# Second expert phase of a two-layer mixture-of-experts kernel: blocks of 288 rows in split F32R, with casting DMAs for the high weight halves

## What is computed

```python
x = x + L0_ffn(L0_cond(x, ...))     # attention with 16 heads, then 16 experts of capacity 128
x = x + L1_ffn(L1_cond(x, ...))     # gated experts over all rows, then the phase of this change

def L1_ffn(x, w_router, w1, b1, w2, b2):        # 8 experts, 256 -> 1024 -> 256, top 2
    probs = softmax(xf @ w_router)
    topk_w, topk_idx = top_k(probs, 2)
    weights = sum(topk_w[..., None] * one_hot(topk_idx, 8), axis=1)
    h = gelu(einsum('te,ieh->tih', xf, w1) + b1)          # tanh form
    out = einsum('tih,ihe->tie', h, w2) + b2
    return sum(out * weights[..., None], axis=1)
```

## Time and profile before

| | us |
|---|---|
| three runs | 954.21, 956.26, 960.77 (median 956.26) |
| the profiled execution, its span from the first to the last instruction | 958.2 |
| PE busy with matmuls | 751.5 (78%) |
| DVE busy | 373.4 (39%) |
| ACT busy | 272.7 (28%) |
| POOL busy | 269.9 (28%) |
| second expert phase, first block's matmul to the last result | 671.58 to 939.07 |

### The profile page before, as it was taken

How to read it: one execution, slowest core, us unless ns; L and a number is a source line. 1 busy time by engine, 2 the same in 40 slices (tenths; PEclk the granted TensorE clock), 3 DMA queues, 4 the chain that set the end, 5 groups by cost and what they waited for, 6 DMA issues and landing times. The chain is left out here.

```text
span 958.2 us, 15240 instructions
## 1 busy us (share of the span) xinstructions
PE 751.5 (78%) x4300; PEld 660.9 (69%) x4301; DVE 373.4 (39%) x1016; ACT 272.7 (28%) x743; POOL 269.9 (28%) x533
## 2 busy tenths in 40 slices
PE   1458777620589999368999999954999999999991
PEld 1357666620479889336888888824999999999991
DVE  3353534458511111196666666646111111111110
ACT  1213414410023233141112111110444544454441
POOL 1122021100034545240001001005444554455442
PEclk9675665555679999787999999987899999999996
DMA  8362191030049996369010010020142454222223
GB/s 257 72 149 44 31 325 49 0 104 7 0 120 318 294 322 169 86 223 324 17 33 16 16 33 17 0 88 6 29 118 50 112 126 123 36 33 38 38 33 104
DMA packets 76904, 94.89 MB, mean 99 GB/s; under 512 B 7856, under 2 KB 68272, under 8 KB 76592
## 3 DMA queue, kind: packets, MB, share of 16 engines
q1 hardware_dynamic: 64000, 77.67, 26.1%
q0 software_dynamic: 10240, 14.32, 8.7%
q10 hardware_dynamic: 2640, 2.62, 0.9%
HBM read 78.39 MB, written 18.10 MB: 101 GB/s over the span
## 5 line engine op out<-in xcount | busy, mean ns | idle before, releaser
L1039 PEld LDWEIGHTS npH<-nXT,w_sb 128*128 128x128 f32 x1152 | 136.4, 195 | 3.2 <-DVE nXT L1070 1.1
L1039 PE MATMUL npH<-nXT,w_sb 128*128 128x128 f32 x1152 | 136.9, 278 | 0.7 <-DVE nXT L1070 0.7
L1047 PE MATMUL npY<-w_sb,nhT 128*128 128x256 f32 x576 | 133.6, 385 | 0.0
L1058 ACT ACT_TABLE_LOAD x40 | 51.3, 1283 | 256.6 <-PE npH L1039 175.6
L1047 PEld LDWEIGHTS npY<-w_sb,nhT 128*128 128x128 f32 x576 | 106.5, 190 | 15.8
L102 POOL TENSOR_TENSOR held<-ones 128x1 f32<-128x1 f32 x212 | 46.0, 217 | 156.2 <-DVE nyg L1087 66.4
L1336 PE MATMUL low_banks<-dw,hid 128*128 128x256 f32 x320 | 77.5, 386 | 4.6 <-DVE hid L1371 4.6
L1058 ACT ACTIVATE nhT<-npH,c_sb 128x128 f32<-128x128 f32 x288 | 78.2, 383 | 0.4
L1310 PE MATMUL f_pt<-xparts,gparts 128*128 128x512 f32 x240 | 72.0, 436 | 2.8 <-ACT uparts L1343 2.8
L1336 PEld LDWEIGHTS low_banks<-dw,hid 128*128 128x128 f32 x320 | 61.5, 193 | 15.5 <-DVE hid L1371 5.4
L1386 DVE SCALAR_TENSOR_TENSOR xc<-low_banks,W,xc 128x256 f32<-128x256 f32 x160 | 66.1, 475 | 2.3 <-PE low_banks L1336 2.3
(11 more groups left out here) (323 smaller groups left out, 965.4 us busy)
## 6 DMA issues: line engine op xcount, KB each, us to landing
w_sb<-in_w SPq DMA_DIRECT2D x32, 1024.0 KB, 8.1
w_sb<-in_v SPq DMA_DIRECT2D x16, 1024.0 KB, 9.8
bias_sb<-in_bias SPq DMA_DIRECT2D x4, 1024.0 KB, 13.3
acc<-zrow SPq DMA_DIRECT2D x1, 2056.0 KB, 17.0
sums<-acc SPq DMA_DIRECT2D x4, 514.0 KB, 5.4
x_sb<-in_x SPq DMA_DIRECT2D x1, 2048.0 KB, 10.1
table<-row ACTq DMA_DIRECT2D x1, 2048.0 KB, 15.5
b_sb<-in_b SPq DMA_DIRECT2D x1, 2048.0 KB, 8.6
```

Source lines behind the costliest of these rows:

```text
L1039: ins = pe.matmul(pH[:, c // 4, (c % 4) * P:(c % 4 + 1) * P], w1_sb[:, u, k, c * P:(c + 1) * P], XT[:, k], start=(k == 0), stop=(k == KD - 1))
L1047: ins = pe.matmul(pY[:, 0:D], hT[:, c], w2_sb[:, u, c], start=(c == 0), stop=(c == FC - 1))
L1058: act.activation(hT[:, c], pH[:, c // 4, (c % 4) * P:(c % 4 + 1) * P], act_fn, bias=b1t[:, ds(e, 1), c]).then_inc(gelu_done, 1)
```

## The change

The second expert phase gets a body of its own in place of expert_phase. The tiles of the dense stage are freed before it.

- Blocks are of WIDE = 288 rows, gathered as NSUB = 3 parts of SUB = 96. The three routing tables have 96 lanes and 75 columns; block numbers come from rounding in f32 instead of integer shifts. In routing, the gate product moves from POOL to ACT, and `ends` goes.
- The transposed form is kept: the weights are stationary in both layers, 288 rows are the moving columns. Each product is three F32R matmuls (low x high, high x low, high x high), in the second layer with w2l, w2h, hh and hl into pY. POOL's scatter(j) waits for yg_ready and issues three DMAs, gather three; gated(j) on DVE waits for y_turned and signals yg_ready. The result is yT (256 wide as 2 x 128 partitions, 288 columns), gets its bias on ACT (Identity), is turned back on PE (turn_back) in the middle of the next block's first layer, and is gated on DVE (gated).
- The hidden tile is split on DVE into hh and hl, two chunks at a time; the gathered columns into xh (ACT) and xl (DVE).
- The weights get four new tiles, w1h, w1l, w2h, w2l, each with two halves for the experts e and e + 1. The high halves of expert 0 are made by ACT (keep_high). Those of experts 1 to 7 are read from HBM a second time by DMAs on POOL's queue that cast f32 to F32R (cast_high). The low halves are made by DVE (low_first, low_second) from the f32 weights in the ring and the high halves. SP reloads a ring slot once the low halves of its expert are made.

```diff
+        def cast_high(pool, e):
+            pool.dma_start(w1h[:, e % 2], v1[e].rearrange("(k p) f -> p k f", p=P)).then_inc(w_cast, 16)
+            pool.dma_start(w2h[:, e % 2], v2[e].rearrange("(c p) d -> p c d", p=P)).then_inc(w_cast, 16)
+        def high_is_there(eng, e):
+            if e:
+                eng.wait_ge(w_cast, 32 * e)
+                eng.wait_ge(w_in[e % RING], 32 * (W_ROUND + 1 + e // RING))
+            else:
+                eng.wait_ge(w_hi, 2)
+        def low_first(dve, e):
+            high_is_there(dve, e)
+            dve.tensor_tensor(w1l[:, e % 2].rearrange("p k f -> p (k f)"), w1_sb[:, e % RING].rearrange("p k f -> p (k f)"),
+                              w1h[:, e % 2].rearrange("p k f -> p (k f)"), ALU.subtract).then_inc(w_lo, 1)
...
+            def per_block(eng, name, body, begin=None):
+                for e in range(E1):
+                    if begin:
+                        begin(eng.snap(reg), e)
+                    n = eng.value_load(nblk[0:1, e:e + 1], min_val=0, max_val=WBLK)
+                    with eng.If(n > 0):
+                        with eng.Fori(0, n):
+                            body(eng.snap(reg), e)
+                            eng.reg_add(reg, reg, 1)
...
+                def _(sp):
+                    sp.sem_inc(gelu_done, FC)
+                    for s in (fc2_done, y_biased):
+                        sp.sem_inc(s, 1)
+                    for e in range(E1 - RING):
+                        sp.wait_ge(w_lo, 2 * e + 2)
+                        load_expert(sp, v1, v2, e + RING, e)
...
+                def _(pool):
+                    gather(0)
+                    cast_high(pool, 1)
+                    pool.dma_start(held[:, 1:2], ones[:, 0:1]).then_inc(scattered, 16)
+                    pool.wait_ge(scattered, 16)
+                    pool.wait_ge(turned, 1)
+                    pool.wait_ge(gathered, 16 * NSUB)
+                    gather(1)
+                    def body(j, e):
+                        scatter(j)
+                        pool.wait_ge(turned, j + 2)
+                        pool.wait_ge(gathered, j * (16 * NSUB) + 32 * NSUB)
+                        held_here(pool, 1)
+                        gather(j + 2)
+                    def begin(j, e):
+                        if 1 <= e and e + 1 < E1:
+                            pool.wait_ge(fc2_done, j + 1)
+                            pool.tensor_tensor(marks[:, e:e + 1], ones[:, 0:1], ones[:, 0:1], ALU.mult)
+                            cast_high(pool, e + 1)
...
+                def _(pe):
+                    def begin(j, e):
+                        pe.wait_ge(w_lo, 2 * e + 2)
+                    def body(j, e):
+                        u = e % 2
+                        pe.wait_ge(x_ready, j + 1)
+                        for c in range(FC):
+                            if c == FC // 2:
+                                turn_back(j)
+                            pe.wait_ge(gelu_done, j * FC + c + 5)
+                            for k in range(KD):
+                                at = slice(c * P, (c + 1) * P)
+                                pe.matmul(pH[:, c % 4, 0:WIDE], w1l[:, u, k, at], xh[:, k], start=(k == 0), stop=False)
+                                pe.matmul(pH[:, c % 4, 0:WIDE], w1h[:, u, k, at], xl[:, k], start=False, stop=False)
+                                ins = pe.matmul(pH[:, c % 4, 0:WIDE], w1h[:, u, k, at], xh[:, k], start=False, stop=(k == KD - 1))
+                            ins.then_inc(fc1_done, 1)
+                        pe.wait_ge(yg_ready, j + 1)
+                        turn(j + 1)
+                        for c in range(FC):
+                            if c % 2 == 0:
+                                pe.wait_ge(h_ready, j * (FC // 2) + c // 2 + 1)
...
+                        ins.then_inc(fc2_done, 1)
...
+                def _(act):
+                    def body(j, e):
+                        for c in range(FC):
+                            act.wait_ge(fc1_done, j * FC + c + 1)
+                            act.activation(h[:, c], pH[:, c % 4, 0:WIDE], ACT.Gelu_apprx_tanh,
+                                           bias=c1_sb[:, e, c:c + 1]).then_inc(gelu_done, 1)
+                        columns(j + 1)
+                        act.wait_ge(fc2_done, j + 2)
+                        act.activation(yT[:, 0], pY[:, 0, 0:WIDE], ACT.Identity, bias=c2_sb[:, e, 0:1])
+                        act.activation(yT[:, 1], pY[:, 1, 0:WIDE], ACT.Identity, bias=c2_sb[:, e, 1:2]).then_inc(y_biased, 1)
...
+                def _(dve):
+                    dve.memset(yT[:], 0.0).then_inc(y_zero, 1)
+                    low_first(dve, 0)
+                    columns(0)
+                    low_second(dve, 0)
+                    def begin(j, e):
+                        if e + 1 < E1:
+                            low_first(dve, e + 1)
+                            low_second(dve, e + 1)
+                    def body(j, e):
+                        for p in range(FC // 2):
+                            if p == FC // 4:
+                                gated(j) 
+                            two = slice(2 * p, 2 * p + 2)
+                            dve.wait_ge(gelu_done, j * FC + 2 * p + 2 + FC)
+                            dve.tensor_copy(hh[:, two], h[:, two]).then_inc(hh_ready, 1)
+                            dve.wait_ge(hh_ready, j * (FC // 2) + p + 1)
+                            dve.tensor_tensor(hl[:, two], h[:, two], hh[:, two], ALU.subtract).then_inc(h_ready, 1)
+                        columns(j + 1)
+                    gated(per_block(dve, "dve", body, begin))
```

More of the change, by code:

```diff
@@ L30 @@
 RING = 4
+SUB = 96
+NSUB = 3
+WIDE = SUB * NSUB
+WBLK = 2 * B * N // WIDE + E1
+WCOLS = NSUB * (WBLK + 3)
+ROUND = 12582912.0
 EPS = 1e-5
@@ L1110, in moe_kernel @@
         c1_sb = sb("c1_sb", [P, E1, FC], into=late)
-        c2_sb = sb("c2_sb", [P, E1, D], into=late)
+        c2_sb = sb("c2_sb", [P, E1, KD], into=late)
         zpad = sb("zpad", [P, D], into=late)
+        dense = ctx.enter_context(ExitStack())
+        xc = sb("xc", [P, T, D], into=dense)
         late_const = sem("late_const")
@@ L1136, in top_two @@
                     link(dve.scalar_tensor_tensor(lg[:], oh[:, 0], -4.0, lg[:], ALU.mult, ALU.add))
-        x1T = sb("x1T", [P, KD, B * N], into=late)
-        xparts = sb("xparts", [P, 2, KD, B * N], F32R, into=late)
+        x1T = sb("x1T", [P, KD, B * N], into=dense)
+        xparts = sb("xparts", [P, 2, KD, B * N], F32R, into=dense)
         NCH, CH = 4, 512
@@ L1517, in moe_kernel @@
             return
[L1521 to L1524, removed]
+        dense.close()
+        w1h = sb("w1h", [P, 2, KD, F0], F32R, into=late)
+        w1l = sb("w1l", [P, 2, KD, F0], F32R, into=late)
+        w2h = sb("w2h", [P, 2, FC, D], F32R, into=late)
+        w2l = sb("w2l", [P, 2, FC, D], F32R, into=late)
+        w_hi, w_lo = sem("w_hi"), sem("w_lo")
@@ new lines, in moe_kernel @@
+        marks = sb("marks", [P, E1], into=late)
+        def cast_high(pool, e):
[7 more added lines that the diff above has]
+                eng.wait_ge(w_hi, 2)
@@ L1639, in _ @@
                     act.activation(lg[:], lg[:], ACT.Exp).then_inc(h_exp, 1)
+                    keep_high(act, 0)
+                    for c in range(NCH):
+                        for n in range(2):
+                            act.wait_ge(b_ready, 2 * c + n + 1)
+                            for t in range(TC * c, TC * c + TC):
+                                ins = act.activation(Bv[:, t, n, 1], Bv[:, t, n, 2], ACT.Copy, scale=best2[:, n, t:t + 1])
+                            ins.then_inc(g_ready, 1)
                 @block.tensor
                 def _(pe):
-                    pe.wait_ge(h_const, 5)
+                    pe.wait_ge(h_const, 4)
                     pe.wait_ge(m_ready, 1)
```

180 lines of the change are left out of this document (135 added, 45 removed).

## The result

The changed kernel takes 1031.68 us (median; 1023.68 to 1032.83), beside 955.24 for the kernel before on the same chip: a ratio of 1.077 [1.071, 1.083]. The profiled run took 1032.15, its span is 1030.2, and 958.2 was the span before. It is 5 us under the forecast of 1037, well inside its range and on the side that it put at 0.90.

The account below looks back on a forecast made before the run. TensorE alone was taken to bound the kernel, with 36 blocks in 267.5 us. The phase's 76.7 us plus the tail's 4.5 made 81 us more, so 1037 us on the median's scale, range 995 to 1095.

Parts of the forecast that it names:

- Blocks: TensorE's work in the expert phase: 16 blocks of 14.3 us, 229 us against 267.5, 38 less if nothing waits.
- The added wait: First block of experts 1 to 6: TensorE idles 14.4 us for yg_ready behind the next expert's cast; 46.0 us per expert.
- T0: The end of the last second layer of expert e-1, from which the steps of expert e are timed.
- clock loss: TensorE after each wait: half-speed clock costs 3 us, with 0 to 6 for the range.
- two bounds, 8 and 14: Landing of POOL's cast pair: 8 us from SyncE's load rate, 14 from the software queue's rate; 11 taken, midway.
- The first expert: Start of the expert phase: first matmul 13.3 us after 664.75, casts landing at 16.6, block two ending at 46.4.
- The tail: After the last block: bias, six transposes back, gated and three scatters for one make the result 4.5 us later.
- The sum: Whole kernel: 76.7 us more in the phase plus 4.5 in the tail, 81 us slower.
- The slow cast: Rival on POOL's loads: conversion and descriptor writing in series take 18 us, giving 1086; chance 0.22.
- The clock did come back: Rival of a clock staying low: 1.2 GHz through the whole next block, some 17 us more per expert, about 1140; chance 0.06.
- Nothing waits: Rival on the expert phase: casts land ahead of VectorE's wait, 25 us faster, 932; chance 0.05.
- The cover: Work on ACT, VectorE, POOL and SyncE hidden under TensorE costs nothing; routing 0, within 2 us either way.

Follow-up runs that it names:

- plain_load: Changed kernel with POOL's casting DMAs replaced by plain f32 loads of the same bytes into spare space: 1029.4 us, 1.068 of the kernel before.
- start_gathered: Changed kernel with VectorE's first weight subtraction waiting until the first three gathers have landed: 1020.6 us, 1.067 of the kernel before.
- more_cast: Changed kernel with a third casting DMA of 1 MB per expert, which VectorE also waits for: 1045.0 us, 1.097 of the kernel before.
- three_high: Changed kernel with a third buffer for the high halves, so casts are issued an expert earlier: 951.3 us, 0.994 of the kernel before.
- low_late: Changed kernel with VectorE making expert e's low halves at the end of expert e-1, an expert later: 946.5 us, 0.990 of the kernel before.
- warm: Changed kernel with 88 extra F32R matmuls before TensorE's yg_ready wait in experts 1 to 6's first block: 1023.8 us, 1.066 of the kernel before.
- start_late: Changed kernel with VectorE waiting for POOL's held operation before its first weight subtraction: 1018.3 and 1033.9 us in two runs, no ratio.

## Why the prediction was right, point by point

**Blocks.** Predicted 0.135 us a matmul and 14.3 a block. Matmuls of the second block start at 748.52, 748.65 and 748.78, so 0.13 (0.133 over the layer); the block is 14.0, 16 of them 224.5 instead of 229. Scaling the 512-column row down by its columns was right to 2%.

**The added wait.** The order of steps was as worked out, and the terms came near, the cast's landing least (us, measured in expert 1's first block from the rows above):

| step | predicted | measured |
|---|---|---|
| T0 to the casts' issue | 2.2 | 3.1 |
| issue to landing | 11 | 8.6 |
| two low subtractions | 4.6 | 4.5 |
| pairs of hh and hl | 2.6 | 2.2 |
| gated, to TensorE's resumption | 1.15 | 1.4 |
| TensorE idle | 14.4 | 12.7 (13.0, mean of six) |
| clock loss | 3 | 2.8 (2.4, mean of six) |
| expert's cycle | 46.0 | 43.4 (mean of six) |

Six cycles are 260.4 instead of 276. The cast is the term that was mis-sized, 11 for 8.6. Of its two bounds, 8 and 14, the lower was the right one: during the cast the core's DMA moves 280 GB/s, and by plain_load the conversion takes 0.2 us at most. The other bound divided bytes by engine time of gathers and scatters, which says how such small rows go, not large loads. By the fit of the Trainium skill (DMA: Bandwidth & Descriptors, Anatomy of one DMA) the pair is estimated at 6.8 us, 1.8 too short; 8.6 lies between it and what I took. The issue of 1280 rows on POOL, bounded at 6 us, took 1.9 for both DMAs. The 2.3 us for a low subtraction was right by luck in part: a straight line through the two rows that were quoted for it (512 elements in 0.685, 256 in 0.35) gives 1.3 ns an element and 2.7 us, and one of the two has a single input; the 1 ns that was taken doesn't follow from them.

**The first expert.** The first matmul came 16.0 after gidx instead of 13.3. I had priced no collision of POOL with VectorE there; the port row explains 2.1 of the 2.7 (start_gathered). From first matmul to expert 1 it took 37.4 instead of 33.1, and here one step failed: the gap before its turn (1.6 us) was put to the cast by way of VectorE; the cast had landed at 682.2, 13.6 before TensorE resumed, and nyg was done at 690.4, before the first layer's end at 691.2. What TensorE waited for, 4.57 us, was the gather of block 1, issued from 686.9 on. Two things made it late. POOL stood 6.3 us in front of it for its small DMA of held, which was queued behind the two casts and landed with them: that is how the cast acts on this expert, and why more_cast (gap 7.7) and three_high (10.3) make it longer. Then POOL's copy and held were each held up by a subtraction, 3.9 us together. low_late has the same casts and the same wait for held (6.4) but no subtraction beside POOL's two operations (0.18 and 0.19), and the gap is gone; so this collision is enough to explain it. start_gathered, which takes the collision away only for block 0, leaves the gap whole (5.2).

**The tail.** 3.2 more instead of 4.5. The terms were those named: bias 0.9, transposes 0.8, nyg 1.3, three scatters at 1.5.

**The sum.** Phase 68.1 more against 76.7, tail 3.2 against 4.5, routing end 0.75 against 0: 72.0 against 81.2. The six cycles were 15.6 too long (six times 1.4 of idle time, twelve blocks of 0.27, six times 0.6 of clock); the first matmul and the first expert were 7.0 too short. That these have opposite signs, and that POOL's late issue (0.9) hides a part of the cast's 2.4, is luck; the path and the order of its steps are not.

**The rivals.** The slow cast is refuted by plain_load. The clock did come back: 1.00 in the block from 749.0 on, and warm shows what its absence cost. "Nothing waits" needed yg_ready before the first layer's end; in the changed kernel it came 12.7 us after. three_high and low_late are that rival made real, and with 951 and 946 us they end on the side it named; its 932 counted no gather that lands late, no 1.3 us restart and a first matmul at 13.3.

**The cover.** ACT's gelus of 288 columns take 0.50 (0.41 predicted) and stayed under TensorE; the work put at nothing was at nothing, but for POOL's small operations while VectorE subtracts and its small DMA of held behind the first casts.

## What to carry to other kernels

When a load is moved to a queue that starts it only after a buffer comes free, ask which engine waits for it first and what stands behind that wait in the engine's own order: here two lines of VectorE's begin stood ahead of an unrelated signal and cost 83 us of a 342 us phase, while with that wait taken away the phase was 15 us shorter than in the kernel before, casts and all. Either consume the load later (low_late) or start it earlier with one more buffer (three_high); both turned 8% slower into 0.6 to 1.0% faster. And look at what else the same queue has behind the load: a small DMA that an engine waits for lands no earlier than the load does (6.3 us behind one pair of casts, 16.6 behind two). Price a wait on TensorE as the idle time and the slow clock behind it, but don't look there for the cause.

## What the runs showed of the hardware

- A casting DMA from f32 to F32R takes hardly longer than a plain one: 8.56 and 8.34 us for two loads of 1 MB (8.73 and 8.65 in the mean of seven), 2.8 for a third.
- An F32R matmul of 288 columns goes every 0.133 us at 2.4 GHz and every 0.24 at 1.2 (first layer of expert 0, starts at 682.39 and 682.63).
- A two-input VectorE subtraction holds up a small POOL operation until it ends (0.2 us becomes 2.1 to 2.6), and also (start_late) the issue of an indirect DMA on POOL's queue (1.01 becomes 2.94), which I had not expected.
- After 12.7 us without matmuls the granted clock was 0.50 for about 6 us of work (738.8 to 744.9); with extra matmuls in the gap it stayed 1.00, but for one expert of six in which 2.3 us of the gap were left empty (1.1 to 1.4 in the others) and it fell to 0.50 for 826.5 to 829.7.
- TensorE starts 1.1 us after the last thing it waited for when that wait is the one for w_lo at an expert's first block (low_late); why it takes so long there no run separates.
